# Reordered tails, an earlier turn into the first stage, and a last queue summed by VectorE, in an attention kernel between two expert layers

## What is computed

```python
x = x + 0.5 * ffn(layernorm(x))        # 8 experts, top 2, at most 640 tokens per expert and choice
x = x + attention(layernorm(x))
x = x + 0.5 * ffn(layernorm(x))        # the same experts again

# ffn: for k in (0, 1): tokens go to the queue of their k-th expert (a queue holds 640)
gate = silu(rows @ wi_gate[e].T); up = rows @ wi_up[e].T
out[token] += share[token, k] * ((gate * up) @ wo[e].T)

# attention, 4 heads of 32 channels; q, k, v = silu(causal_conv4(h @ W))
delta = delta_rule(l2norm(q), l2norm(k), v, sigmoid(h @ Wb))   # per chunk of 32 the inverse of a
                                                               # triangular 32x32, then a scan of states
ms = channel_mix(kernel_mix(conv3(v), conv15(v), conv31(v)))   # "lags" of v
w = softmax(gelu([h, mean|ms|, mean|delta|, mean|v|] @ w1 + b1) @ w2 + b2)
o = w0 * ms + w1 * delta + w2 * v
out = rmsnorm(o) * o_norm_w @ Wo
```

## Time and profile before

| | |
|---|---|
| runs of the kernel | 917.56 us median (915.59 to 918.95, 3 runs) |
| the profiled execution | 912.17 us |
| its span, first to last instruction | 910.4 us |
| mean granted TensorE clock | 0.964 of 2.4 GHz |
| busy | PE 92%, DVE 60%, ACT 43%, POOL 55% of the span |
| opening of the attention, to its first solve | 262 to 332 us |
| regular tails | 392 to 419, 489 to 517, 586 to 613 us |
| experts e2 | 706 to 910 us |

### The profile page before, as it was taken

The page is one execution under the profiler, slowest core; times in us unless marked ns, Lnnn a source line. Parts: engine busy times, 40 slices in busy tenths (PEclk is TensorE's granted clock), DMA queues, the critical chain, the costliest instruction groups (busy, mean ns, idle before and its releaser), DMA issues. The chain is left out here.

```text
span 910.4 us, 26331 instructions
## 1 busy us (share of the span) xinstructions
PE 840.4 (92%) x10927; PEld 744.3 (82%) x10927; DVE 544.5 (60%) x1634; ACT 393.0 (43%) x850; POOL 504.6 (55%) x631
## 2 busy tenths in 40 slices
PE   8679999999969789999999999988978999999996
PEld 7559999999957566787668777876867999999996
DVE  5835655655457936676585836484462666665662
ACT  5834444444314522474436633752441544444431
POOL 2768889866620821682148534864434434336667
PEclk7779999999989899999999999999988999999998
DMA  9843877444231110012001310112112544445544
GB/s 309 152 115 112 258 239 218 130 122 132 61 96 42 27 37 12 4 33 58 9 4 30 86 38 30 31 27 71 42 65 82 200 155 154 127 128 125 116 64 36
DMA packets 75508, 85.97 MB, mean 94 GB/s; under 512 B 9800, under 2 KB 62196, under 8 KB 74365
## 3 DMA queue, kind: packets, MB, share of 16 engines
q1 hardware_dynamic: 61180, 63.74, 23.7%
q0 software_dynamic: 14208, 20.55, 9.9%
HBM read 46.70 MB, written 34.01 MB: 89 GB/s over the span
## 5 line engine op out<-in xcount | busy, mean ns | idle before, releaser
L1044 DVE TENSOR_TENSOR e_hid<-e_sg,e_pu 128x320 f32<-128x320 f32 x256 | 124.8, 488 | 159.2 <-ACT e_sg L985 154.6
L985 ACT ACTIVATE e_sg<-e_pg 128x320 f32<-128x320 f32 x256 | 112.0, 438 | 207.8 <-PE e_pg L942 207.7
L283 POOL DMA_INDIRECT queue<-wide_rows,slot x64 | 67.9, 1061 | 84.5 <-PE a_po L1596 20.5
L1136 POOL TENSOR_TENSOR first_rows<-a_inv,a_nmat 128x135 f32<-128x135 f32 (+20 forms) x116 | 61.6, 531 | 67.4 <-DVE a_nmat L1989 59.0
L940 PE MATMUL e_pg<-e_xlo,e_whi 128*128 128x320 f32 x256 | 96.1, 375 | 0.8 <-DVE e_xlo L1007 0.8
L928 PE MATMUL e_po<-e_expert,e_hid 128*128 128x128 f32 x640 | 83.7, 275 | 1.3 <-DVE e_hid L1044 1.3
L928 PE MATMUL e_po<-expert,e_hid 128*128 128x128 f32 x640 | 84.2, 274 | 0.0
L928 PEld LDWEIGHTS e_po<-e_expert,e_hid 128*128 128x128 f32 x640 | 79.9, 191 | 1.8 <-DVE e_hid L1044 1.8
L928 PEld LDWEIGHTS e_po<-expert,e_hid 128*128 128x128 f32 x640 | 80.3, 191 | 0.1
L941 PE MATMUL e_pg<-e_xhi,e_wlo 128*128 128x320 f32 x256 | 79.3, 310 | 0.0
L942 PE MATMUL e_pg<-e_xhi,e_whi 128*128 128x320 f32 x256 | 79.1, 309 | 0.0
(11 more groups left out here) (381 smaller groups left out, 2084.4 us busy)
## 6 DMA issues: line engine op xcount, KB each, us to landing
expert<-wexp_in SPq DMA_DIRECT2D x14, 512.0 KB, 4.5
e_expert<-wexp_in SPq DMA_DIRECT2D x14, 512.0 KB, 4.3
line<-blank SPq DMA_DIRECT2D x3, 1310.0 KB, 7.5
e_xs<-queue SPq DMA_DIRECT2D x12, 327.5 KB, 4.8
e_xs<-line SPq DMA_DIRECT2D x6, 647.5 KB, 6.8
expert<-wexp_in SPq DMA_DIRECT2D x14, 256.0 KB, 2.8
e_expert<-wexp_in SPq DMA_DIRECT2D x14, 256.0 KB, 2.8
queue<-blank SPq DMA_DIRECT2D x2, 1310.0 KB, 9.5
```

Source lines behind the costliest of these rows:

```text
L283: pool.indirect_dma_start(io.queue, bass.IndirectOffsetOnAxis(ap=k.slot[:, j, 1:2], axis=0), k.xn[:, j, :], None, bounds_check=SLOTS - 1, ...
L985: act.activation(sg[n % 2][:], pg[n % 2][:, 0:HALF], ACT.Silu).then_inc(silued, 1)
L1044: dve.tensor_tensor(hid[q % 2][:, f, c * HALF:c * HALF + HALF], sg[n % 2][:], pu[n % 2][:, 0:HALF], ALU.mult).then_inc(hidden, 1)
L1136: link(eng.tensor_tensor(part, bc(inv[:, j:j + 1, own], shape), bc(factor, shape), ALU.mult))
```

## The change

In the attention's opening, 40 idle matmuls stand where 56 stood, and 10 new ones stand ahead of the lags. The inversion of group 0 is split at column 6. VectorE's second `low_values` stands behind seven steps instead of ten, and `low_rows(1)` inside the inversion, ahead of its last six steps. In all stages the terms of a lag go high by high, high by low, low by high, and a group's first lag waits for `vhigh` alone, its third matmul for `vlow`. In the regular tails ScalarE does square and root of half 2g ahead of the second exponential, and `keep_mixture(2g)` ahead of `keep_stacked`; VectorE does `rescale(2g)` ahead of `cross_values`; TensorE issues 12 lag matmuls instead of 20 ahead of `turn_mixture(2g)`. In e2 the last queue's indices are made early out of a load of their own (`ahead`), what its tokens' rows hold by then is gathered into `rest`, VectorE adds it, and the last five stores are plain.

The diff, cut:

```diff
@@ experts: SyncE
                     load_rows(q + 2)
+                if not raw and q + 2 == E:
+                    sp.dma_start(ahead[:], io.queue[SLOTS - CAP:SLOTS, D:ROW].rearrange(
+                        "(s p) d -> p s d", p=P)).then_inc(peeked, 16)
@@ experts: VectorE
-                if half and q // E in BY_TOKEN:
-                    index(q)
+                if half and q // E in BY_TOKEN and (raw or q < LAST):
+                    index(q, rows_of(q)[:, :, D:ROW])
...
-                    if not raw:
+                    if not raw and q == LAST:
+                        dve.wait_ge(foretold, 1)
+                        dve.wait_ge(restored, 16 * CT)
+                    elif not raw:
                         dve.wait_ge(indexed, numbered(q))
...
-                elif q < E:
+                elif q < E or q == LAST:
                     dve.scalar_tensor_tensor(rows[q % NR][:, s, :], down_bank(tile), factor[:, q, s:s + 1],
-                                             rows_of(q)[:, s, ROW:WIDE], ALU.mult, ALU.add).then_inc(rready, 1)
+                                             rows_of(q)[:, s, ROW:WIDE] if q < E else rest[:, s, :],
+                                             ALU.mult, ALU.add).then_inc(rready, 1)
...
+                    if not raw and q + 1 == E and n == REST_AT:
+                        dve.wait_ge(peeked, 16)
+                        index(LAST, ahead[:])
@@ experts: GpSimd
-                    put = deliver if raw else replace if q < E else add_up
+                    put = deliver if raw else replace if q < E or q == LAST else add_up
...
                 all_stored(pool, 0)
+                pool.wait_ge(foretold, 1)
+                for s in range(CT):
+                    gather(pool, io.out, token[:, LAST, s:s + 1], rest[:, s, :], restored)
+                pool.wait_ge(restored, 16 * CT)
                 keep_tiles(CT * E, CT * NQ)
@@ attention
-        SPLIT = 8
+        SPLIT = 6
+        ROWS_IN = 25
@@ attention: TensorE, scales
                     elif first:
-                        pe.wait_ge(silued, UNITS * a + 6 - bank)
+                        pe.wait_ge(vhigh, 2 * a + 2)
+                    if i == TERMS - 1 and not half:
                         pe.wait_ge(vlow, 2 * a + 2)
...
-                        x, w = ((vhi, k.lag_hi), (vlo, k.lag_hi), (vhi, k.lag_lo))[term]
+                        x, w = ((vhi, k.lag_hi), (vhi, k.lag_lo), (vlo, k.lag_hi))[term]
@@ attention: TensorE, stage
+                if not here:
+                    keep_clock(pe, k, pp[:, 0, :], 10)
                 part = filler(6)
...
-                part = filler(20 if here else SCALES)
+                part = filler(12 if here else SCALES)
...
-            keep_clock(pe, k, pp[:, 0, :], 56)
+            keep_clock(pe, k, pp[:, 0, :], 40)
@@ attention: VectorE
                     low_values(a, 0)
-                    invert_first(5, 10)
+                    invert_first(5, 7)
                     low_values(a, 1)
+                    invert_first(7, 10)
                     cross_values(a)
-                    invert_first(10, CHUNK - 1)
+                    invert_first(10, ROWS_IN)
+                    low_rows(g + 2, 0)
+                    low_rows(g + 2, 1)
+                    invert_first(ROWS_IN, CHUNK - 1)
...
+                if here:
+                    rescale(2 * g)
                 if ahead and here:
                     cross_values(a)
                 if here:
-                    rescale(2 * g)
                     mixture(2 * g + 1)
...
-                if later:
+                if later and here:
                     low_rows(g + 2, 0)
-                if later:
                     low_rows(g + 2, 1)
@@ attention: ScalarE
+                if here and ahead:
+                    ask_for(ACT.Sqrt)
+                    square(2 * g)
+                    root_mix(2 * g)
+                    power(2 * g + 1)
+                    ask_for(ACT.Sqrt)
+                    keep_mixture(2 * g)
+                if here and not ahead:
                     square(2 * g)
                     power(2 * g + 1)
                     root_mix(2 * g)
+                    keep_mixture(2 * g)
                 if ahead:
                     keep_stacked(2 * a)
-                if here:
-                    keep_mixture(2 * g)
-                if ahead:
                     keep_near(2 * a)
```

More of the change, by code:

```diff
@@ L775, in experts @@
         downed, rready, indexed = sem("downed"), sem("rready"), sem("indexed")
+        peeked, foretold, restored = (None if raw else sem(n) for n in ("peeked", "foretold", "restored"))
         stored = [[sem(f"stored{i}") for i in range(NR)], k.delivered] if raw else k.stored
@@ L782, in experts @@
         NB = 2 * FT
+        rest = None if raw else sb("rest", [P, CT, D])
+        ahead = None if raw else sb("ahead", [P, CT, ROW - D])
         DOWN_AT = (2, 3, 4, 5, 6)
@@ L1024, in evacuate, with index @@
                                       ALU.mult).then_inc(rready, 1)
[L1026 to L1027 removed]
+            def index(q, row):
                 if raw:
[L1029 removed]
+                    dve.tensor_scalar(token[:, q, :], row[:, :, 0], float(APART), None, ALU.add).then_inc(indexed, 1)
                 else:
[L1031 removed]
+                    dve.tensor_copy(factor[:, q, :], row[:, :, 1 + q // E])
                     spare = C_TRASH + q % 2 * CT
[L1033 to L1034 removed]
+                    dve.scalar_tensor_tensor(token[:, q, :], row[:, :, 0], float(2 * APART),
+                                             k.const[:, spare:spare + CT], ALU.add,
+                                             ALU.min).then_inc(foretold if q == LAST else indexed, 1)
             low_weights(0, 0)
@@ L1076, in keep_tiles @@
                     if s == 0:
[L1077 removed]
+                        if raw or q < LAST:
+                            pool.wait_ge(indexed, numbered(q))
                         if not raw and q % E >= 2:
@@ L1118, in _ @@
                 all_stored(pool, c)
-        return range(wgot[0].num, (stored[0][NR - 1] if raw else indexed).num + 1)
+        return range(wgot[0].num, (stored[0][NR - 1] if raw else restored).num + 1)
 def behind(eng, sem, value):
```

9 lines of the change are left out of this document (1 added, 8 removed).

## The result

The changed kernel takes 909.19 us (median of 7 runs, 907.3 to 910.21), the kernel before 915.96 us on the same chip (7 runs, 912.98 to 918.95). The ratio is 0.9924 (95% interval 0.9904 to 0.9945), so the change saves 7.0 us (0.76% of 915.96), with 5.0 to 8.8 us as bounds. The forecast was 9.2 us of a gain and 908.4 us; the range held the time. The sign was right, the size of the gain was put 2.2 us too high. That the time itself lies only 0.8 us from the forecast is in part luck: the median of the kernel before, on which the forecast was built, was 917.56 us in its first three runs and is 915.96 us in all seven.

The account below looks back on a forecast made before the run. TensorE, busy 92% of the span, was taken as the bound. Terms -1.0 - 5.3 + 0.2 - 3.1 = -9.2 us take the profiled 912.17 to 902.97 us, or 908.4 from the 917.56 median; range 903.5 to 913.5.

Parts of the forecast that it names:

- A: Attention's opening: 40 idle matmuls instead of 56 let the first transposes start with their data, -1.0 us (bounds 0 to -1.6).
- Rival 5: Opening: fewer idle matmuls leave a hole, the clock stays at 1.2 GHz through 78 projections, 14.8 us slower, 923.2; chance 4%.
- B: Turn from opening to stage 0: earlier lags, split at column 6, solve then waits for the inverse, -5.3 us.
- a step grows by 0.0045 us per element: Group 0's inversion on VectorE: six columns instead of eight save 2.1 us over the 21 steps from row 10.
- a clock of 0.50 in the opening: Sign that would prove the forecast wrong: TensorE at 1.2 GHz in the attention's opening.
- rival 3: Turn into stage 0: low rows inside the inversion stall VectorE or stacked copies land late; gain only 2 us, 911.7; chance 12%.
- C: Tails of the three regular stages: the new order only moves TensorE's wait, +0.2 us in all (bounds -2.1 to +3.9).
- stages as long as before within 0.5 us: Expected sign for the reordered regular tails: stage lengths unchanged within 0.5 us.
- Rival 1: Regular tails give back their waits and something on top, -2.1 us, 906.1 in all; chance 15%.
- Rival 2: Regular tails: ScalarE's extra table change costs a full switch, delaying `a_z` copies; +1.4, +0.7 and 0, 910.5; chance 12%.
- D: End of the kernel: gathered rows let the last queue's five stores be plain, -3.1 us (bounds -2.1 to -3.7).
- The cover: Last queue: GpSimd's slack, 2.9 us made up per queue, hides the gathers' delay; two queues are enough.

Follow-up runs that it names:

- e12: The kernel before with the new regular tails alone; turn into stage 0, idle matmuls and last queue as before: ratio 1.0029 (1.0002 to 1.0056) to the kernel before.
- e1: The changed kernel with the turn into stage 0 as before (split at 8, no ten idle matmuls, old lag order): ratio 0.9939 to the kernel before.
- e4: The changed kernel with only the inversion's split put back to column 8: ratio 0.9904 to the kernel before.
- e10: The changed kernel with the split at column 8, run again in a later set: 902.45 us, ratio 0.9910 to the kernel before.
- e11: The changed kernel with the split at column 8 and the regular tails as before: 900.38 us, ratio 0.9902 to the kernel before.
- e2: As a run: the changed kernel with the regular tails as before on all three engines: ratio 0.9904 to the kernel before.
- e3: The changed kernel with the last queue stored as before, with sums in memory: ratio 0.9948 to the kernel before.
- e5: The changed kernel with the inversion split at column 7: ratio 0.9905 to the kernel before.

## Why the prediction was right, and where it was off

**A, -1.0 us: right, at the upper end.** The opening's first projections start 9.44 us behind the first idle matmul in the changed kernel, 10.53 before, 1.09 less, and VectorE's idle 0.98 us is gone. In e12, with 56 idle matmuls, the clock rose earlier and they came at 9.96; so A is 0.5 to 1.1 us, by when the clock rises. Rival 5 fell: the opening's projections still start every 0.237 us.

**B, -5.3 us: the mechanism held up to the channel matmuls, one step was mis-sized.** Third lag, end of the lags, clock there, stacked copies came as worked out, and GpSimd's last step ended 57.3 us behind the mark (forecast 58.3). The step that failed is "a step grows by 0.0045 us per element; the 21 steps from row 10 on lose 462 elements, 2.1 us". The two rows behind that slope were measured with GpSimd beside VectorE and without it. The slope was taken for the price of elements and was the price of company. With two more columns on GpSimd, rows 10 to 24 went from 11.90 us to 13.43 instead of to about 10.0. `xlo` came late, the hole of 3.02 us brought the clock down (a clock of 0.50 in the opening was one of the forecast's own signs of being wrong), and the keys, which the forecast had ending ahead of the inverse, became what ends last: 65.1 to 65.9 for the solve instead of 62.7. B was -2.4 us (e1). It is rival 3's place and nearly its size (-2), by another cause: VectorE was not stalled, it was slowed. With SPLIT put back to 8 and the rest of the edit kept, B gives 5.2 us (67.96 less 62.75, the mean of e4, e10 and e11).

**C, +0.2 us: the tails as worked out, the stages not.** "The wait at the first transposes turns into one at the second" is what the rows show, 1.54 us against 1.52 in sum where the small instruction takes the same time. The sign "stages as long as before within 0.5 us" did not come: 1.75 us, from the heads. Rival 1 (-2.1) is refuted by e2 and e12. Rival 2 had copies later by 1.2 us in each stage, and the time by 1.4 and 0.7 us in the first two; but the channel matmuls come 14.38, 14.67 and 14.35 us behind the second half's first hidden layer, before 14.43, 14.77 and 15.43. The table loads stand at 1.28 us with no drain behind them. The Trainium skill, "ScalarE: Activation LUTs", section "What ACT_TABLE_LOAD costs", gives about 1283 ns for the load, which these rows bear out, and a drain that makes about 2.66 us of a switch, which they do not show. The three comparisons of times (e2 against the changed kernel, e11 against e10, e12 against before) all lean to a cost, of 2 to 3 us, and only e12's interval leaves out zero, narrowly. Where it would lie is open. Between the solves, the three profiled executions with old tails average 283.0 us, the eleven with new ones 284.3. Of that the three tails make 0.2 (64.1 and 64.3), the heads, in which the tails' edit moves nothing, 1.1 (218.9, from 217.8 to 220.4, and 220.0, from 218.1 to 222.6). That is inside the scatter of the heads. A cost by the place of the code was not tried.

**D, -3.1 us: right.** -2.8 us by the marks (202.57 in e3, 199.8 in the others): 1.8 from the last store's start, 1.1 from its landing. The gathers delayed the stores by 4.6 us more than forecast and GpSimd caught up in more than three queues, not two. The cover was large enough.

In sum, with A at -0.8, B at -2.4 and D at -2.8, the parts make -6.0 us without the tails; the two ratios of the changed kernel say -7.0 and -4.4. The over-forecast is B's, by 2.9 us, and perhaps C's. The second ratio's 4.4 us would be less than half of the gain that was forecast. The range's lower end, 903.5, is 0.5 us below its own sum (917.56 - 13.6 = 904.0), which changes nothing here.

The best version found is the split at column 8 with the rest of the change, at 0.9904 and 0.9910; with the tails as before it is 0.9902, not to be told from it. Its lead over the changed kernel rests on the marks (2.8 us), as the intervals of the two ratios overlap.

## What to carry to other kernels

A duration read beside another engine's work includes that work. Before dividing labour anew between VectorE and GpSimd, look whether the rows that give the price were taken with both running, and count what the one pays for the other's added columns. When an engine's wait is shortened by an early start, ask whether the next wait grows long enough to lose the clock. And in a program of 900 us, marks inside the trace show differences of 0.5 us that the total hides behind 6 to 12 us of scatter.

## What was not expected of the hardware

- VectorE's 126-element instruction takes 0.28 us alone and 0.56 beside GpSimd's steps; 15 steps take 8.4 us alone (302.52 to 310.92), 11.9, 12.6 and 13.4 beside GpSimd with 23, 24 and 25 columns. It is GpSimd's share that sets VectorE's pace, more than VectorE's own columns.
- A hole of 3.02 us cost eight matmuls at 1.2 GHz, one of 2.05 us (e5) as many, a filled one none; holes of 1.35 us ahead of the lags and 1.19 ahead of the keys cost nothing. The hole of 5.60 us before the change cost thirteen.
- Waits named issue come to between 0.2 and 3.0 us in the head of a stage, at other places from kernel to kernel. Less these waits, the three heads together, where their clock stands at 1.00, agree to 0.9 us.
- In the tail of stage 1 an instruction of 128x48 on VectorE took 0.28 us in three executions and 0.61 to 0.64 in ten, and in twelve of these thirteen the tail was 21.3 or 21.95 us long with it.
